# A filter's down product with the data as the stationary operand, and a new split of the median's counts

## The reference, cut to what matters

```
q_in = jnp.quantile(x.reshape(B, C, -1), 0.5, axis=-1)
x = x + jax.nn.relu(-q_in)[:, :, None, None]
y = upfirdn2d(x, lpf, up=2, padding=6, gain=4.0)
y = jnp.maximum(y, 0.0)
x = upfirdn2d(y, lpf, down=2, padding=0, gain=1.0)
spec = jnp.fft.rfft2(x, norm='ortho')
mag = jnp.abs(spec)
gate = sigmoid(fg_w2 @ gelu(fg_w1 @ mag))
xf = x + jnp.fft.irfft2(spec * gate, norm='ortho')
out = attention(q(xf), kv(conv8(xf)), kv(conv16(xf))) @ proj_w + proj_b + x
```

## Time and profile before

| what | value |
|---|---|
| time, median of 3 | 11593.28 us |
| span of the profiled execution (no other time of it is given) | 11587.8 us |
| PE busy | 10430.9 us, 90% |
| PEld busy | 5268.4 us, 45% |
| DVE busy | 8781.7 us, 76% |
| ACT busy | 7244.9 us, 63% |
| POOL busy | 2762.1 us, 24% |
| mean granted clock of TensorE | 0.980 |

### The profile page before, as it was taken

How to read it: one execution, slowest core, us unless ns; L and a number is a source line. 1 busy time by engine, 2 the same in 40 slices (tenths; PEclk the granted TensorE clock), 3 DMA queues, 4 the chain that set the end, 5 groups by cost and what they waited for, 6 DMA issues and landing times. The chain is left out here.

```text
span 11587.8 us, 198556 instructions
## 1 busy us (share of the span) xinstructions
PE 10430.9 (90%) x71885; PEld 5268.4 (45%) x72029; DVE 8781.7 (76%) x15079; ACT 7244.9 (63%) x12109; POOL 2762.1 (24%) x5218
## 2 busy tenths in 40 slices
PE   1898998989989899899989989899898998989989
PEld 1544535344453544535445354443534445354453
DVE  6877778777777777778777787777777777777776
ACT  5657566675656757567575666756567565675756
POOL 2312213122131221312223131321312213122130
PEclk9999999999999999999999999999999999999999
DMA  2021220212213022130211302122121221302213
GB/s 61 24 46 47 45 66 25 50 39 51 60 31 59 28 50 56 36 61 34 42 52 42 69 20 47 46 48 63 29 49 35 52 60 31 59 31 49 55 37 74
DMA packets 176570, 537.72 MB, mean 46 GB/s; under 512 B 64872, under 2 KB 87400, under 8 KB 154032
## 3 DMA queue, kind: packets, MB, share of 16 engines
q1 hardware_dynamic: 175664, 525.31, 20.1%
HBM read 232.49 MB, written 71.30 MB: 26 GB/s over the span
## 5 line engine op out<-in xcount | busy, mean ns | idle before, releaser
L978 DVE TENSOR_REDUCE R<-ps 128x2 f32<-128x640 f32 x4096 | 3182.3, 817 | 889.4 <-PE ps L714 888.1
L1185 ACT ACTIVATE R<-ps 128x512 f32<-128x512 f32 x5120 | 2819.2, 594 | 646.8 <-PE ps L735 621.6
L258 ACT ACTIVATE R<-R,st 128x1475 bf16<-128x1475 f32 (+1 forms) x1326 | 2077.1, 1566 | 489.9 <-DVE st L330 465.1
L319 DVE TENSOR_SCALAR_CACHE_REDUCE R<-R,st 128x1255 bf16<-128x1255 f32 (+1 forms) x1326 | 1936.4, 1460 | 18.6 <-DVE st L330 0.2
L714 PE MATMUL ps<-KST,R 96*128 96x320 bf16 x8192 | 1802.2, 301 | 40.6 <-DVE R L978 31.0
L760 PE MATMUL ps<-R 128*32 128x512 f32 x12288 | 1638.8, 606 | 38.0 <-DVE Wk L931 32.8
L735 PE MATMUL ps<-R,KST 104*128 104x512 bf16 x4096 | 1563.0, 384 | 38.6 <-ACT R L1185 23.1
L714 PEld LDWEIGHTS ps<-KST,R 96*128 96x128 bf16 x8192 | 754.3, 98 | 727.4 <-DVE R L978 215.1
L1268 POOL CAST R<-Wk 128x512 bf16<-128x512 f32 x256 | 283.7, 1108 | 2477.3 <-DVE Wk L931 2477.3
L735 PEld LDWEIGHTS ps<-R,KST 104*128 104x128 bf16 x4096 | 394.2, 97 | 724.4 <-ACT R L1185 458.6
L384 POOL TENSOR_TENSOR R<-R,sB 128x1024 f32<-128x1024 f32 x136 | 255.1, 1897 | 1642.7 <-DMA R<-xh_in 1637.3
(11 more groups left out here) (210 smaller groups left out, 19138.3 us busy)
## 6 DMA issues: line engine op xcount, KB each, us to landing
R<-R SPq DMA_DIRECT2D x3072, 64.0 KB, 2.4
R<-xh_in SPq DMA_DIRECT2D x136, 512.0 KB, 4.5
out_dram<-Z SPq DMA_DIRECT2D x68, 1024.0 KB, 3.9
R<-xa_in SPq DMA_DIRECT2D x36, 1024.0 KB, 11.4
R<-xb_in SPq DMA_DIRECT2D x36, 1024.0 KB, 12.0
R<-sr_in SPq DMA_DIRECT2D x32, 1024.0 KB, 5.4
R<-sr_in SPq DMA_DIRECT2D x16, 2016.0 KB, 9.2
R<-sr_in SPq DMA_DIRECT2D x16, 1056.0 KB
```

The costliest lines, as they stand in the source:

```text
L258: e.activation(junka[:, 0:o2 - o1], xc[:, o1:o2], ACT.Sign, bias=mid, scale=-1.0, accum_out=ca[i]).then_inc(md_ca, 1)
L319: e.tensor_scalar(junk[:, 0:o1 - o0], xc[:, o0:o1], mid, None, ALU.is_le, ALU.add, accum_out=cv[i]).then_inc(md_cv, 1)
L978: e.tensor_reduce(MX[(4 * u + s4) % 2][:, blk_, h0:h0 + 2], ps[:, 2 + 2 * bq:4 + 2 * bq, 0:320], axis=AX.X, op=ALU.max).then_inc(mx, 1)
L1185: e.activation(PB[:, t % 2, w, :], ps[:, w % 2, :], ACT.Exp).then_inc(ex, 1)
```

## The change

The down product now has a 128 by 128 block of Y as stationary operand and the taps (64 columns) as moving operand. Its result has rows and columns exchanged, as the turning made them before, so VT, its copy on VectorE (L849), the turnings (L517) and the semaphores `vt` and `tr_ps` are gone. There are eight matmuls a pair instead of two, into bank 4 or 5 in turn. The copy to V (L863) reads that bank in the round after the product. The VectorE share of a count piece goes from 0.46 to 0.54 in the first 21 steps (from 1255 or 1256 columns to 1474).

```
-MIDS = [[a + int((0.46 if k < 21 else 0.36) * (b - a)) for a, b in zip(CUTS, CUTS[1:])] for k in range(STEPS)]
+MIDS = [[a + int((0.54 if k < 21 else 0.36) * (b - a)) for a, b in zip(CUTS, CUTS[1:])] for k in range(STEPS)]
...
-        VT = [R1[:, 3112 + 512 * i:3624 + 512 * i] for i in range(2)]
...
                 m = n - 2
                 if 0 <= m < P:
                     e.wait_ge(yr, m + 1)
-                    if m:
-                        e.wait_ge(vt, m)
-                    for j in range(2):
-                        op = e.matmul(ps[64 * j:64 * j + 64, 4, :], lhsT=c(f"d{j}"), rhs=Y[m % 2][:, j, :],
-                                      start=True, stop=True)
+                    if m > 1:
+                        e.wait_ge(vv, m - 1)
+                    for i in range(4):
+                        for j in range(2):
+                            op = e.matmul(ps[:, 4 + m % 2, 128 * i + 64 * j:128 * i + 64 * j + 64],
+                                          lhsT=Y[m % 2][:, j, 128 * i:128 * i + 128], rhs=c(f"d{j}"), start=True, stop=True)
                     op.then_inc(dn_ps, 1)
...
-                m = n - 3
-                if 0 <= m < P:
-                    e.wait_ge(vt, m + 1)
-                    if m:
-                        e.wait_ge(vv, m)
-                    for i in range(4):
-                        op = e.transpose(ps[:, 5, 128 * i:128 * i + 128], VT[m % 2][:, 128 * i:128 * i + 128], c("ident"))
-                    op.then_inc(tr_ps, 1)
...
-                m = n - 2
-                if 0 <= m < P:
-                    e.wait_ge(dn_ps, m + 1)
-                    if m > 1:
-                        e.wait_ge(tr_ps, m - 1)
-                    e.tensor_copy(VT[m % 2], ps[:, 4, :]).then_inc(vt, 1)
...
-                    e.wait_ge(tr_ps, m + 1)
+                    e.wait_ge(dn_ps, m + 1)
                     if gq > 1:
                         e.wait_ge(z_ps, gq - 1)
                     e.tensor_copy(V[gq % 2][:, :, o:o + 2, :],
-                                  ps[:, 5, :].rearrange("p (c h n) -> p h c n", c=2, h=2)).then_inc(vv, 1)
+                                  ps[:, 4 + m % 2, :].rearrange("p (c h n) -> p h c n", c=2, h=2)).then_inc(vv, 1)
```

More of the change, by code:

```diff
@@ L51 @@
 SIGNALS = (
-    "up_ps t1 tm yw_ps yr dn_ps vt tr_ps vv vr z_ps zz xr ru_ps rt rw_ps ry rd_ps rb mw_ps my mb mv_ps mq mz_ps mzz zcl zst0 zst1 zst2 zst3 zad "
+    "up_ps t1 tm yw_ps yr dn_ps vv vr z_ps zz xr ru_ps rt rw_ps ry rd_ps rb mw_ps my mb mv_ps mq mz_ps mzz zcl zst0 zst1 zst2 zst3 zad "
     "md_v md_max md_p md_cv md_ca md_r md_fs md_g md_lift md_ends md_raise md_ta md_tb md_got md_mm md_row md_end "
@@ L149, in program @@
         RS = [W[:, 1536 + 512 * i:2048 + 512 * i] for i in range(2)]
-        (up_ps, t1, tm, yw_ps, yr, dn_ps, vt, tr_ps, vv, vr, z_ps, zz, xr, ru_ps, rt, rw_ps, ry, rd_ps, rb,
+        (up_ps, t1, tm, yw_ps, yr, dn_ps, vv, vr, z_ps, zz, xr, ru_ps, rt, rw_ps, ry, rd_ps, rb,
          mw_ps, my, mb, mv_ps, mq, mz_ps, mzz, zcl, zst0, zst1, zst2, zst3, zad,
@@ L548, in tensor @@
                     else:
-                        e.wait_ge(vt, P)
                         e.wait_ge(vv, P)
```

## The result

The changed kernel takes 11,849.32 us (median of 4 runs, 11,828.06 to 11,865.94) beside 11,597.17 for the kernel before: ratio 1.0219, 95% interval 1.0205 to 1.0233, slower. It was forecast at 11,785 with a range of 11,670 to 11,880. Its profiled execution has a span of 11,846.2 us, 258.4 above the one before.

What follows compares the result with a forecast made beforehand. TensorE was taken to bound the filter stage to some 93%. Terms of 8.5 + 0.9 + 2.0 + 0.5 = 11.9 us an image, x 16 = 190, + 8 = 198, gave 11,791, rounded to 11,785; range 11,670 to 11,880.

Steps and rivals of the forecast that it cites:

- Record price 0.11, product 1.94: Down product on TensorE: 0.11 us a record, set by the weight load, so 1.94 us to the next product.
- Part of the product hidden, filter +8.5: Filter stage: 14 us more TensorE work an image, 5.5 hidden in its waits, so 8.5 us longer.
- Drain +0.9: Drain between filter and Fourier stages: ten longer VectorE counts +2.3, two copies less -1.4, +0.9 us an image.
- Fourier +2.0: Fourier stage: 13 longer VectorE counts at 0.23, less about 1.0 idle, +2.0 us an image, between 0 and 3.9.
- Behind it +0.5: Three counts behind the Fourier stage: +0.5 us an image, between 0 and 0.7.
- lone median +8: Median at the program's start: +0.4 us a step over 21 steps, +8 us once, between 0 and 14.
- copy 0 in the filter stage: Removing VectorE's 687 ns copy L849 gives nothing in the filter stage, where VectorE has 20 us to spare.
- The copy V's waits over when reached: New copy to V and the product's wait for an earlier copy: both waits already over when reached.
- A: Rival, chance 0.12: TensorE's waits move and don't shrink; filter +14 us an image, 11,900 us in all.
- B: Rival, chance 0.09: all waits swallowed, Fourier stage stays at TensorE's pace; +6.5 us an image, 11,697 us.
- C: Rival, chance 0.07: narrower stream makes a record cheap, 0.06 us; product 1.13 instead of 1.60 us (even), 11,553 us.
- D: Rival, chance 0.02: weight load and stream don't overlap; 0.17 us a record, product 2.9 us, 12,280 us.

Runs made afterwards that it cites:

- experiment 7: Changed kernel with 128 instead of 64 moving columns in each of the down product's eight matmuls; 11,870.15 us.
- experiment 4: Changed kernel with 64 already met waits (32 instructions) added in TensorE's part ahead of the loop over images; 11,812.37 us.
- experiment 2: Changed kernel with its new product but the VectorE share of the counts at 0.46 as before; 11,824.98 us, ratio 1.0201.
- 10: Changed kernel with each down matmul cut into two 64-column weight halves in turn, 32 padding instructions ahead of TensorE's loop, VectorE share 0.46; 11,493.90 us.
- 11: Changed kernel with down matmuls cut into halves in turn, padding ahead of the loop, VectorE share 0.54 in the first 10 steps, then 0.46; 11,449.78 us.

## Why the prediction was right, and where not

The direction, the size and the range were right; the middle was 64 us low. By its own steps:

- **Record price 0.11, product 1.94** (even pair +0.35, odd +0.5): right, 1.94 measured. The reason given (the load sets it) is shown by experiment 7: the stream does not. L446 was the right nearest row.
- **Part of the product hidden, filter +8.5**: right in sum. With before's restart place (experiment 4) the stage is 133.1 us, +8.5, and +8.1 in the images without a cold round; in the changed kernel it is +10.2, and the cold rounds are the excess. The two terms, 14 of work less 5.5 of waits, are not confirmed one by one: PE's idle time in rounds 3 to 30 fell from 5.7 to 2.5 us an image, by 3.1. Since this counts a record's latency as busy it is a lower bound of the waits, but it suggests that both terms were too large. That the split helps to hide (count 0.18 shorter on ACT) is right too: 1.3 us by experiments 2 and after in undisturbed images, 3.0 by 10 and 11.
- **Drain +0.9**: wrong, +3.1. The step put ten counts at 0.23 and took off 1.4 for two copies. The split alone costs 3.9 there; 1.8 of it is the minimum L323 waiting for GpSimd twice, a shift of phase that no count of instructions shows. The product alone gives only 0.3 back (26.7 us in experiment 2): the copies that go stand beside waits for PE's longer products, as in DVE's row of the changed kernel:

```profile
1125.89 0.08 DVE L318 DVE_READ_ACCUMULATOR R<-R,st 128x1 f32 x1
1129.28 0.69 DVE L841 COPY Z<-ps 128x512 f32<-128x512 f32 x1 [3.31 <-PE ps L508]
```

The prediction had named DVE the chain of the whole drain; in its first 5 us PE is.
- **Fourier +2.0**: too high, +0.8. Three periods take 8.38 us, not 8.7. From the earlier trace rows, 8.20 before; the split alone adds 0.15 to the stage, where PE's pace covers the counts. With the new product it adds 1.3 (experiment 2 against the changed kernel), and the product alone takes 0.5 off. The sum is within the stated 0 to 3.9.
- **Behind it +0.5, lone median +8, copy 0 in the filter stage**: right (+0.5, +8.1; DVE's wait of 90.5 us for L498 is 1.0).
- **The copy V's waits over when reached**: right, 8.4 us in all 512.
- **The term that was missing** is the restart: 2.1 us of pause at the loop's back edge and some 1.9 of cold rounds an image, 62 us in all, as much as the forecast was low. That the two agree so well is luck: the drain's 2.2 us an image too little (35 us) are made up by the Fourier stage's 1.2 too much (19), the 0.8 of the inverse transform that no run explains (13) and 0.3 in the filter. I had the trace of before with its 1.84 us pause and the change in the number of instructions, and counted instructions only as work. Padding took it away and, on the kernel before, brought it on.
- **The rivals.** A (+14 in the filter) not: waits shrank; PE's waits for ACT's L1064 fell from 54.4 to 24.8 us in all. B not: the Fourier stage did stay near PE's pace, but the filter grew by 8, not 6; its sum also leaves out the 8 us of the lone median. C named the right thing at the wrong operand: a narrow stream does not make a record cheap while the weights are 128 wide (experiment 7), narrow weights in turn do, and then the kernel is faster. D not.

## What to carry to other kernels

A float32 matmul with full-width weights and few moving columns paid for its load here; with the weights cut into the two column halves and issued in turn, the same product took 1.08 us instead of 1.94. A change in the number of TensorE's instructions can move a loop's end to a place where the branch back waits 2 us longer for its instructions and the clock is low behind it: look at the duration of the branch and at the first products behind it before a stage is blamed, and try a padding ahead of the loop. Where one engine's share of split work grows, price it stage by stage: where that engine is the chain it is paid in full.

## What the runs showed that I had not expected

- 32 records in 1.01 us in turn, 1.76 in one column half.
- 224 idle instructions ahead of a loop cost 35 us (0.37%) in a loop that they don't touch, by a restart of 6.31 instead of 4.15 us and 15 instead of 2 cold starts.
- The clock fell a second time, in rounds 5 and 6 of 6 of 16 images of experiment 2, at 4.8 us each; in the same kernel with padding it did so in one.
- A minimum of a single column on VectorE took 0.15 to 1.23 us, by where it fell in a GpSimd instruction.
